# One product of queries and keys for two tiles, in fp32r, with the signature a tile further ahead

## The reference

```
h = signature(path, depth 4) @ W.T + b                 # running path signature, 128 outputs per step
h = h + attention(layernorm(h), w_qkv, w_out, ...)     # 8 heads of 64, spectrally normed weights, no self-attention
h = h + ffn(layernorm(h), gate, w1, w2, w3, sw1, sw2)  # 8 experts, top-1 routing, and a shared GELU expert
```

## Time and profile before

| | |
|---|---|
| median of 3 runs | 641.4 us |
| the profiled execution | 641.93 us |
| its span | 640.1 us |
| mean granted TensorE clock | 0.995 |
| busy share: TensorE, VectorE, GpSimd, ScalarE | 96%, 67%, 50%, 45% |
| tile 0 starts | 41.87 us |
| tile 31 starts | 471.64 us |
| first products of the routed experts | 528.86 us |

### The profile page before, as it was taken

How to read it: one execution, slowest core, us unless ns; L and a number is a source line. 1 busy time by engine, 2 the same in 40 slices (tenths; PEclk the granted TensorE clock), 3 DMA queues, 4 the chain that set the end, 5 groups by cost and what they waited for, 6 DMA issues and landing times.

```text
span 640.1 us, 13350 instructions
## 1 busy us (share of the span) xinstructions
PE 615.5 (96%) x4085; PEld 517.7 (81%) x4085; DVE 428.1 (67%) x1093; ACT 289.6 (45%) x640; POOL 320.9 (50%) x336
## 2 busy tenths in 40 slices
PE   6889999999999999999999999999989999999993
PEld 4667888887888887888888787888768999999992
DVE  6977767767777766777776678788556535666450
ACT  4334444544444445343444434444465445666341
POOL 2365544554544454554455455445864502666663
PEclk9999999999999999999999999999999999999998
DMA  8620433344543334343334434111233732434330
GB/s 303 240 106 21 107 82 82 86 117 93 114 116 82 82 97 114 85 108 90 82 82 109 105 90 108 38 37 39 70 93 98 233 105 64 54 58 52 43 47 2
DMA packets 69901, 59.80 MB, mean 93 GB/s; under 512 B 6512, under 2 KB 58608, under 8 KB 69488
## 3 DMA queue, kind: packets, MB, share of 16 engines
q1 hardware_dynamic: 63232, 55.21, 33.3%
q0 software_dynamic: 6640, 4.22, 4.8%
HBM read 16.79 MB, written 26.30 MB: 67 GB/s over the span
## 4 chain that ended last, share of the span: by engine, by line
PE 87%; DVE 6%; POOL 3%; issue 2%; ACT 1%; DMA 0%; SPq 0%; DVEq 0%; POOLq 0%
PE bank L1303 80%; PE bank L1515 2%; PE bank L1360 2%; POOL sorted_rows L510 1%; POOL z L495 1%; POOL z L497 1%; DVE z L923 1%; PE bank L1618 1%; DVE whigh L818 1%; PE bank L1409 1%; PE bank L1418 0%; DVE h L822 0%; PE bank L1364 0%; DMA h<-x_prev 0%; DVE u L868 0%
## 5 line engine op out<-in xcount | busy, mean ns | idle before, releaser
L1303 PE MATMUL bank<-whigh,uth 128*128 128x512 f32 x512 | 167.3, 407 | 1.5 <-issue 1.3
L1303 PEld LDWEIGHTS bank<-whigh,uth 128*128 128x128 f32 x512 | 91.7, 189 | 27.2 <-issue 8.1
L1303 PE MATMUL bank<-whigh,utl 128*128 128x512 f32 x256 | 101.2, 395 | 0.0
L584 POOL DMA_INDIRECT out<-xvo,ids x39 | 61.5, 1577 | 62.9 <-ACT xvo L773 55.8
L504 POOL TENSOR_TENSOR rstd<-rstd,powers 128x1 f32<-128x1 f32 x64 | 35.3, 551 | 113.7 <-DVE rstd L910 65.6
L495 POOL TENSOR_TENSOR z<-z 128x512 f32<-128x512 f32 x32 | 40.8, 1275 | 70.5 <-DVE z L923 70.5
L1303 PE MATMUL bank<-xT,qkw 128*128 128x128 f32 x512 | 63.3, 277 | 0.0
L659 ACT ACTIVATE prob<-prob 128x512 f32<-128x512 f32 x32 | 20.2, 633 | 93.3 <-DVE prob L1050 93.3
L1303 PEld LDWEIGHTS bank<-xT,qkw 128*128 128x128 f32 x512 | 59.6, 192 | 0.7 <-issue 0.4
L1303 PEld LDWEIGHTS bank<-whigh,utl 128*128 128x128 f32 x256 | 48.1, 188 | 11.3
L490 POOL TENSOR_TENSOR e3l<-e,e3h 128x512 fp32r<-128x512 f32 x31 | 40.0, 1292 | 26.8 <-DVE xn L944 26.4
(11 more groups left out here) (236 smaller groups left out, 1364.6 us busy)
## 6 DMA issues: line engine op xcount, KB each, us to landing
sorted_rows<-blank SPq DMA_DIRECT2D x24, 709.5 KB, 6.1
xvp<-xvo SPq DMA_DIRECT2D x128, 128.0 KB, 2.3
w<-w_t SPq DMA_DIRECT2D x1, 4096.0 KB, 12.1
w<-w_high SPq DMA_DIRECT2D x4, 512.0 KB, 6.3
x_columns<-x2t SPq DMA_DIRECT2D x32, 64.0 KB, 1.6
xg_in<-x_columns SPq DMA_DIRECT2D x8, 256.0 KB, 4.1
out<-h SPq DMA_DIRECT2D x8, 256.0 KB, 2.2
levels<-w_t SPq DMA_DIRECT2D x1, 2048.0 KB, 10.5
```

The lines of the kernel that those rows point to most:

```text
L584: nc.gpsimd.indirect_dma_start(out=out[:, :], out_offset=bass.IndirectOffsetOnAxis(ap=ids[:, tile:tile + 1], axis=0), in_=y[:, 2 if j == S ...
L1303: return T.matmul(out_, lhsT, rhs, start=start, stop=stop)
```

## The change

- The queries' product is made once for two tiles, in the even tile: 8 heads, each as three fp32r products of 256 columns (both tiles' split columns side by side). `qkw` is split into high part and remainder at the start (one ScalarE cast, one GpSimd subtraction of 1024 columns). Each bank holds two heads for both tiles, so banks 5 and 6 are filled twice; ScalarE empties them in four copies, and its copies of the values stand between these.
- In an odd tile no queries' product is issued: the router is TensorE's first instruction.
- The tile's x must be known one tile earlier. So the signature (`features`, level 3), the projection, the tree, the first layer norm and `x_columns` all run one tile further ahead; a function `lead` does the additional tile in the start, on each engine.
- `e3` shares its buffer with `u4`; GpSimd's level 3 waits for the transposes of the features before, instead of the level-3 sum. Other buffers move to make room (`xg_in`, `oh_early`, `gelu`).
- The loops on TensorE, ScalarE and VectorE have two tiles in their body; from tile 24 or 26 on the tiles are written out.
- The shared expert begins a tile earlier: group 0's `up` in tile 29, group 1's in tile 30, group 2's in tile 31, each `down` a tile later.

The core of the diff, TensorE's list first:

```diff
+            def queries(heads):
+                for hd in heads:
+                    by_head = B[5 + hd // 2 % 2][:].rearrange("p (a h k) -> p h a k", a=4, h=2)
+                    last = three(by_head[:, hd % 2, :, :], [qkw[:, n, place(hd), :] for n in range(2)], x_pair)
+                    if hd % 2 == 1:
+                        last.then_inc(g_psum, 1)
+            def lead():
+                project(2, 0, 1)
+                accumulate(1)
+                project(2, 1, 5)
+                x_columns(1)
+                project(2, 5, 8)
+                sum_level3(3)
+                project(2, 8, 10)
+                features(3)
+            def iteration(i, par, f, u, acc, prev=True, older=True):
...
-                for hd in range(HEADS):
-                    by_head = B[5 + hd // 4][:].rearrange("p (s h k) -> p h s k", s=2, h=4)
-                    last = mm(by_head[:, hd % 4, :, :], qkw[:, place(hd), :], xT[:])
-                    if hd % 4 == 3:
-                        last.then_inc(g_psum, 1)
+                if par == 0:
+                    pe.wait_ge(xT_hi, 2 * i + 4)
+                    pe.wait_ge(xT_lo, i + 2)
+                    queries(range(4))
...
                     router(i - 2)
-                pe.wait_ge(xT_lo, i + 1)
                 if prev and older:
                     pe.wait_ge(h2_done, i - 1)
                 three(B[7][:], x, [vow[:, n, 0:512] for n in range(2)]).then_inc(vo_psum, 1)
-                pe.wait_ge(g_sb, 2 * i + 1)
-                three(B[5][:], x, [vow[:, n, 512:] for n in range(2)]).then_inc(vo_psum, 1)
-                if u:
-                    project(i + 2, 0, 1)
+                if par == 0:
+                    pe.wait_ge(g_sb, 2 * i + 1)
+                    queries(range(4, 6))
+                    pe.wait_ge(g_sb, 2 * i + 2)
+                    queries(range(6, 8))
+                    if u:
+                        project(i + 3, 0, 1)
+                    pe.wait_ge(g_sb, 2 * i + 3)
+                three(B[6 if is_tile(i, LAST) else 5][:], x, [vow[:, n, 512:] for n in range(2)]).then_inc(vo_psum, 1)
+                if par and u:
+                    project(i + 3, 0, 1)
                 if acc:
-                    accumulate(i + 1)
-                pe.wait_ge(g_sb, 2 * i + 2)
+                    accumulate(i + 2)
+                if par == 0:
+                    pe.wait_ge(g_sb, 2 * i + 4)
...
-                    project(i + 2, 1, 5)
+                    project(i + 3, 1, 5)
-                if is_tile(i, LAST_BUT_ONE):
+                if is_tile(i, LAST_BUT_TWO):
                     pe.wait_ge(z_sb, 2 * TILES)
                     pe.wait_ge(sw_lo, 1)
-                    up(0, 0, range(HC - 1), True)
+                    up(0, range(HC - 1))
+                if is_tile(i, LAST_BUT_ONE):
+                    down(0, range(2))
+                    up(1)
                 if is_tile(i, LAST):
-                    down(0, 0, range(2), True)
-                    up(1, 1, range(HC - 1))
+                    up(2, range(2))
+                    down(1, range(2))
+                    up(2, range(2, HC))
```

ScalarE's list of a tile:

```diff
-                for n in range(2):
-                    a.wait_ge(g_psum, 2 * i + (n + 1))
-                    A.activation(xqk[:, :, 4 * n:4 * n + 4, :],
-                                 B[5 + n][:].rearrange("p (s h k) -> p s h k", s=2, h=4),
-                                 ACT.Copy, scale=fac[:, 1:2]).then_inc(g_sb, 1)
+                if par == 0:
+                    queries(i, range(2))
...
+                values_out(i, 0, prev)
+                if par == 0:
+                    queries(i, range(2, 4))
+                values_out(i, 1, prev)
...
+                if is_tile(i, LAST_BUT_TWO):
+                    a.wait_ge(tree, 3 * TILES - 2)
+                    gelus(0, range(HC - 1))
+                    x_group_hi(1)
                 if is_tile(i, LAST_BUT_ONE):
-                    a.wait_ge(tree, 3 * TILES - 2)
-                    gelus(0, 0, range(HC - 1))
+                    keep_x2(LAST_BUT_TWO)
+                    gelus(1, range(2))
```

GpSimd's level 3, and the start of the loops on TensorE:

```diff
             def level3(s):
-                pool.wait_ge(s3_psum, s)
+                pool.wait_ge(u4_psum, s)
...
             features(2)
+            lead()
...
+            with pe.Fori(2, RANK_AT, 2) as i:
+                iteration(i, 0, True, True, True)
+                iteration(i + 1, 1, True, True, True)
+            for i in range(RANK_AT, TILES):
+                iteration(i, i % 2, i + 4 < TILES, i + 3 < TILES, i + 2 < TILES)
```

More of the change, by code:

```diff
@@ L78, with shared_bank @@
 PRODUCT_STEP, OUT_COLUMN_STEP, SUMS_STEP, SQUARED_STEP = 1, 3, 4, 5
+def shared_bank(g):
+    return 5 if g == 0 else 6 - g % 2
 def spread(ap, axis, shape):
@@ L239, in taker @@
             return take
[L241 to L244, removed]
+        xqk_even, xqk_odd = (xqk[:, t, :, :, :].rearrange("p a b c -> p (a b c)") for t in range(2))
+        late = taker(levels[:, EXPERTS * HC * DIM:], xqk_odd,
+                     xvo[:].rearrange("p a b c -> p (a b c)"), prob[:].rearrange("p a b -> p (a b)"),
+                     z4[:].rearrange("p a b -> p (a b)"), xvp[:].rearrange("p a b c -> p (a b c)"))
+        z_flat = z[:].rearrange("p c d -> p (c d)")
         w2 = levels[:, 0:EXPERTS * HC * DIM].rearrange("p (e c d) -> p e c d", e=EXPERTS, c=HC)
@@ L639, in iteration, with values_out @@
                                  ACT.Copy, scale=fac[:, 1:2]).then_inc(g_sb, 1)
[L640 to L649, removed]
+            def values_out(i, n, prev):
+                a.wait_ge(vo_psum, 2 * i + (n + 1))
+                if n == 0 and prev:
+                    a.wait_ge(xv_moved, 64 * i)
+                bank = 7 if n == 0 else 6 if is_tile(i, LAST) else 5
+                A.copy(xvo[:, n, :, :].rearrange("p c d -> p (c d)"), B[bank][:]).then_inc(vo_sb, 1)
@@ L650, in iteration @@
                 if f:
[L651 to L652 removed]
+                    low_features(i + 4)
+                if prev and older and not is_tile(i, LAST):
                     keep_x2(i - 2)
                 if f:
[L655 removed]
+                    level3_hi(i + 4)
+                if is_tile(i, LAST_BUT_ONE):
+                    gelus(0, range(HC - 1, HC))
                 if is_tile(i, LAST):
[L657 removed]
+                    gelus(1, range(2, HC))
@@ L747, in expert_hi @@
+            iteration(LAST_BUT_TWO, 1, False, True)
+            iteration(LAST_BUT_ONE, 0, False, False)
+            iteration(LAST, 1, False, False)
+            gelus(2, range(2, HC))
+            keep_x2(LAST)
+            x2_transposed(LAST)
+            x_group_hi(4)
+            for g in range(3, GROUPS - 2):
+                gelus(g)
+                x_group_hi(g + 2)
             def expert_hi(j):
@@ L1228, in _ @@
             assert n_route == ROUTE_STEPS
-            for g in range(1, GROUPS - 3):
-                add_shared(g, g % 2)
+            for g in range(2, GROUPS - 3):
+                add_shared(g)
                 if g + 4 < GROUPS:
-                    x_group_lo(g + 4, g % 2)
+                    x_group_lo(g + 4)
             def expert_weights(j):
@@ L1422, in router, with up, down @@
                 mm(B[4][:, P:P + EXPERTS], x2t[:], gateT[:]).then_inc(lg_psum, 1)
-            def up(g, k, chunks=range(HC), first=False):
+            def up(g, chunks=range(HC)):
                 pe.wait_ge(xg_lo, g + 1)
                 for c in chunks:
-                    if not first:
+                    if g:
                         pe.wait_ge(gelu_done, g * HC + (c + 1 - HC))
-                    three(B[c][:], [sw1[:, n, col(c)] for n in range(2)], (xgh[k], xgl[k])) \
+                    three(B[c][:], [sw1[:, n, col(c)] for n in range(2)], (xgh[g % 2], xgl[g % 2])) \
                         .then_inc(up_psum, 1)
-            def down(g, k, tiles=range(GROUP), first=False):
+            def down(g, tiles=range(GROUP)):
                 pe.wait_ge(gelu_done, (g + 1) * HC)
-                if not first:
-                    pe.wait_ge(added, g - 1)
+                if g:
+                    pe.wait_ge(added, max(g - 1, 1))
                 for t in tiles:
                     for c in range(HC):
-                        last = mm(B[5 + k][:, col(t)], gelu[k][c][:, col(t)], sw2[:, c, :],
+                        last = mm(B[shared_bank(g)][:, col(t)], gelu[g % 2][c][:, col(t)], sw2[:, c, :],
                                   c == 0, c == HC - 1)
@@ L1601, in _ @@
             mm(B[7][:, 0:rest * EXPERTS], ones, oh.rearrange("p t e -> p (t e)")).then_inc(rank_psum, 1)
-            down(1, 1, range(2, GROUP), True)
-            with pe.Fori(2, GROUPS - 3, 2) as g:
-                up(g + 1, 1)
-                down(g, 0)
-                up(g + 2, 0)
-                down(g + 1, 1)
+            down(2, range(2, GROUP))
+            for g in range(3, GROUPS - 2):
+                up(g + 1)
+                down(g)
             def expert(j):
```

369 lines of the change are left out of this document (197 added, 172 removed).

## The result

The changed kernel takes 669.0 us where the kernel before took 641.6 in the same comparison: a ratio of 1.0433, 95% interval 1.0418 to 1.0447. Slower, as forecast, but by 27 us and not by 14; 655.7 was predicted, with a range that ended at 663. The profiled execution is the longest of the three; it spans 669.2 us, 29.1 more than before.

The account below looks back on a forecast made before the run. TensorE's own instructions were taken to bound the tile loop (busy 96% of the span). Product -10.7, odd tiles +12.9 and +5.5, start +3.0, end +3.6 gave +14.3 us, forecast 655.7 us, range 647 to 663.

Parts of the forecast that it names:

- part 5: The end, tiles 29 to 31: ScalarE late with GELUs and query copies; net cost 3.6 us, between -1 and 6.
- part 4: The start: one tile's signature and projection move there; cost 3.0 us, between 1.5 and 4, new weights' remainder at nothing.
- Part 3: Odd tiles: TensorE waits for transposed x2, then nearly for GpSimd's tree; 1.17 each, 12.9 us, plus 5.5 in other tiles.
- Part 1: Queries' product: 24 fp32r products per pair take 2.95 instead of 3.62 us; 10.7 us saved over 16 pairs.
- Part 2: Even tiles: ScalarE empties the twice-filled banks in time, so the copies cost nothing, with a margin of 0.25 us.
- The idle 3.4: In the start, after the features, TensorE idles 3.4 us until VectorE finishes the last operand of tile 2's projection.
- The 1.2 of idle time: Idle time of about 1.2 us said to stand in the same stretch of the start in the kernel before.
- A: Rival: tree and x2 come early enough, odd tiles run on without the 18.4 us of waits; 637 us, chance 0.07.
- E: Rival: an fp32r product of 256 columns is as dear as one of 512; near 700 us, chance 0.02.
- B: Rival: TensorE also waits in even tiles on late ScalarE copies, 0.5 in each of 15; 663 us, chance 0.09.
- C: Rival: the products are bound by columns alone, a pair taking 2.84; 1.8 us less, 654 us, chance 0.07.
- D: Rival: the end goes as laid out, TensorE's new work filling all gaps; 4 us less, 651 us, chance 0.13.

Follow-up runs that it names:

- experiment 3: The kernel before, plus one unread 128x1024 GpSimd subtraction beside VectorE's remainders of the signature's weights, awaited by TensorE ahead of tile 0: 643.4 us, ratio 1.0031.
- experiment 5: Two kernels from the changed one, in odd tiles: router behind both value products, 665.1 us; previous tile's values product moved to the tile's start, 663.3 us.
- Experiment 1: The changed kernel with pairing undone, each tile making its own queries in 16 fp32 passes, lead and end kept: 658.0 us, ratio 1.0248.
- experiment 6: The changed kernel with VectorE adding the shared expert's first group at the start of its tile 31 list instead of the end: 661.9 us, ratio 1.0321.
- experiment 4: The changed kernel with unread products (12 of 128 columns, 13 of 512) filling two idle TensorE stretches in the start: 667.8 us, ratio 1.0414.
- experiment 7: The changed kernel with four repairs: queries' remainder on VectorE, values first in odd tiles, early shared-expert addition, start's idle stretches filled: 653.3 us, ratio 1.0188.

## Why the prediction was right and wrong

The direction and the cause in the odd tiles were right; the sum was about half of what came. Three steps failed, by size: part 5 followed only ScalarE's list through the end (5.1 us for a wait on VectorE and the products behind it), part 4 priced TensorE's idle time without the products behind it at half rate (3.9), and it put the remainder of the new weights at nothing (2.2 in the profile, 2.0 by experiment 3).

**Part 3, the odd tiles: right in what they wait for first.** One wait on ScalarE's x2t copy in each odd tile, and a second chain close behind it: experiment 5 shows that freeing the router gives back 0.36 of it and no more. But that chain is mostly another than the one I named: VectorE's remainder of the features held TensorE for 0.69, GpSimd's tree only for the last 0.1, where I had 0.99 for the tree. The price of the first wait was 1.27 and not 1.17: the idle time begins when the transpose of x2 has been issued, 0.1 ahead of the point from which I counted. Tiles 25 and 27 waited like the others, 1.1, and not 1.8 and 1.6.

**Part 1, the product: right for the 24 products (1.52 + 1.44 = 2.96, forecast 2.95), too good for the seam around them.** In the loop it is 0.23 to 0.29 from the transpose of x2 to the first query, 0.25 in the mean, where it was 0.11. This goes with the place where TensorE's loop begins again, and not with the kinds of product: in the tiles that are written out the same product follows the same transpose after 0.03, as here in tile 28.

```profile
461.93 0.27 PE L1471 MATMUL bank<-sq,x2n 128*128 128x128 f32 x1
461.96 0.36 PE L1356 MATMUL bank<-xTh,qkw 128*128 128x256 f32 x1
462.17 0.28 PE L1356 MATMUL bank<-xTl,qkw 128*128 128x256 f32 x1
```

Experiment 1's kernel, which also has two tiles in its loop, loses some 0.15 at the same place with fp32 queries (0.14 to 0.20 to the first and 1.88 for the product, against 0.11 and 1.78 in the odd tile behind it); the kernel before, with one tile in its loop, shows 0.11 there and in its tiles that are written out alike. Why two tiles in the loop cost this is open. The odd tile's router costs 0.07 more, 0.21 instead of 0.14. So a pair gains 0.66 and loses 0.14, 0.07 and 1.27: it should be 0.82 longer, and it is 0.79 (28.63 against 27.84); forecast 0.50.

**Part 2, the even tiles: right.** No wait at the copies before tile 30.

**Part 4, the lead: the mechanism right, and two things left out.** The idle 3.4 came as 3.33. (The 1.2 of idle time that I took off is 0.8 in the rows, 0.3 ahead of the projection's first part and 0.5 ahead of the sum, and it stood behind the start of tile 0, so in the next stretch of the table.) The first step that failed here is the one that put "the cast and the remainder of the new weights" at nothing. It looked for GpSimd's idle time only, and did not ask what VectorE does beside it. VectorE's remainders took 2.31 and 5.67 instead of 1.23 and 3.50, and TensorE's wait for the values' weights ended at 31.02 instead of 28.86, 2.2 later; experiment 3 prices one such subtraction alone at 2.0 us in the kernel before. The Trainium skill has the rule, "SBUF — State Buffer", section "Who interferes with whom": a VectorE instruction with two inputs in SBUF contends with a GpSimd instruction that reads SBUF. The remainders are of this kind, and the rows agree: 3.50 without, 5.20 and 5.67 with GpSimd beside them, and GpSimd's additions from 0.46 to 1.32 in the other direction.

The second omission is the clock. I priced the idle time as so many us of idleness, and not the products behind it at half rate. From the end of the first wait to the last product ahead of the second it is 15.5 us, and 12.9 in experiment 6's kernel, where the clock held: 2.6. From the end of the second wait to the queries it is 10.7, and 9.4 in the kernels of experiments 4 and 7, where the clock held there: 1.3. Behind the 3.3 us wait, in every profile that has it, the granted clock fell to 0.50. The Trainium skill, "TensorE: Matmul & The Clock Gate", section "HAM oscillation — how this bites in real kernels", describes waits of TensorE after which the next products run at half rate; experiment 4 agrees, 1.00 with the gaps filled.

**Part 5, the end: mis-sized.** The copies of the queries in tile 30 cost 1.1 where I had 1.7 + 0.8, and the exponential of tile 31 shows no wait, where I had 2.0. Instead the addition of the first group held TensorE 3.4 us, and the products behind it at half rate took 1.7 more (experiment 6 gave back 5.3). The step that failed: I had followed ScalarE's queue through these tiles and not VectorE's, although the diff puts both first groups into one bank and the addition at the end of the list.

The rivals: A and E are out (the odd tiles wait, the products cost 0.12 apiece); of B nothing was seen; C is out, as the products took 2.96 a pair and not 2.84, and D too, as the end came out 4.0 above the forecast and not 4 below. The range ended at 663 because each term was bounded by itself and none had the clock in it.

## What to carry to other kernels

Before work is put into an engine's idle time, look at what the other engines do in that time, operands included: a subtraction that ran for free on GpSimd made VectorE's 2 us longer. Price an idle stretch of TensorE with the products behind it, at both clock levels, and look at every engine whose list ends in something that frees a bank. And when a cheaper instruction leaves a hole, ask what it was hiding: the odd tiles gave back more than both tiles saved.

## What the runs showed of the hardware

VectorE and GpSimd slow each other at subtractions and additions from memory: three of 128x1024 went from 3.50 to 5.20 and 5.67 us; GpSimd's 128x128 addition from 0.46 to 1.32.

Behind the same wait of 2.0 us in the start, in kernels that are alike up to there, the granted clock fell in some profiled executions (0.64 to 0.80 from 30 to 36 us in three) and held at 1.00 in two others; behind the wait of 3.3 us it fell to 0.50 in all seven. In tile 29, behind waits of 1.1 and 1.2 us, it fell in experiment 6's kernel (484.6 to 488.0 us) and not in the changed one. So a kernel with such waits has a spread of its own: 667.9 to 671.0 here, 661.7 to 669.2 with the router late, against 641.0 to 642.4 for the kernel before. What decides between the two is open.

Where TensorE's loop of two tiles begins again, the first product came 0.23 to 0.29 us behind the transpose ahead of it, in the changed kernel and in those of experiments 5, 6 and 7; in the tiles written out it came after 0.03, and with one tile in the loop, before the change, after 0.11, the same as in the tiles written out there. The fp32r products of 256 columns followed each other at 0.12.
